# Two feed-forwards interleaved with a state scan: order of the scan's loads and of the first silu, and the place of a sum over weights

## The reference, cut to what matters

```python
x = x + tanh(g_ffn[0]) * L0_ffn(layernorm(x))   # stage 1: silu(gate) * up, two largest of each four kept, down
x = x + tanh(g_xattn[1]) * L1_xattn(...)        # stage 2
x = x + tanh(g_ffn[1]) * L1_ffn(layernorm(x))   # stage 3: h = silu(g * gate_s) * (u * up_s); down * down_s
x = x + tanh(g_xattn[2]) * L2_xattn(ctx, layernorm(x))  # stage 4: gates the result of the scan below
x = x + tanh(g_ffn[2]) * L2_ffn(layernorm(x))   # stage 5: weights rounded to fp8
# L2_xattn: for each of 16 states n, over time t
state = state * exp(delta_t * A[n]) + (delta_t * u_t) * B_t[n];   y_t += state * C_t[n]
# L3_ffn (stage 7) scales its weights by mean(|w|)
scale = 1.0 / clip(mean(abs(w)), EPS)
```

## Time and profile before

| | us |
|---|---|
| median of 3 runs | 4199.0 (4193.92 to 4204.99) |
| the profiled execution | 4200.43 |
| its span in the profile | 4198.9 |
| PE busy | 3734.7 (89%) |
| DVE busy | 3069.5 (73%) |
| ACT busy | 1683.8 (40%) |
| POOL busy | 669.8 (16%) |

### The profile page before, as it was taken

How to read it: one execution, slowest core, us unless ns; L and a number is a source line. 1 busy time by engine, 2 the same in 40 slices (tenths; PEclk the granted TensorE clock), 3 DMA queues, 4 the chain that set the end, 5 groups by cost and what they waited for, 6 DMA issues and landing times.

```text
span 4198.9 us, 41456 instructions
## 1 busy us (share of the span) xinstructions
PE 3734.7 (89%) x12733; PEld 1940.3 (46%) x12786; DVE 3069.5 (73%) x4986; ACT 1683.8 (40%) x2649; POOL 669.8 (16%) x647
## 2 busy tenths in 40 slices
PE   5988888989999998999984999899999999998656
PEld 3555655644444444444432444454554554553222
DVE  6787778768889788888898554575574673774887
ACT  4767676632333322433331011254352452551322
POOL 1433333433333110333210000000000000000000
PEclk8999999999999999999996999899999999999887
DMA  3323232424242322444432000221121110110000
GB/s 106 118 91 114 91 115 85 170 109 151 89 154 85 137 81 91 157 154 153 160 113 88 1 0 0 81 71 53 36 71 36 54 64 25 63 56 33 10 10 20
DMA packets 92131, 346.25 MB, mean 82 GB/s; under 512 B 12160, under 2 KB 20480, under 8 KB 78496
## 3 DMA queue, kind: packets, MB, share of 16 engines
q1 hardware_dynamic: 61888, 226.90, 15.1%
q0 software_dynamic: 30048, 116.94, 8.0%
HBM read 281.40 MB, written 62.39 MB: 82 GB/s over the span
## 4 chain that ended last, share of the span: by engine, by line
PE 55%; DVE 25%; issue 10%; ACT 6%; DMA 3%; POOL 0%; DVEq 0%; ACTq 0%; SPq 0%; POOLq 0%
PE ps L994 36%; PE ps L1339 5%; PE ps L1068 4%; PE ps L1329 3%; PE ps L1216 2%; DVE room L1491 2%; PE ps L1164 2%; DVE room L1495 2%; PE ps L1061 1%; DVE room L1499 1%; DMA room<-bc_scratch 1%; DVE stat L1453 1%; DVE room L1504 1%; DVE stat L1955 1%; DVE room L1960 1%
## 5 line engine op out<-in xcount | busy, mean ns | idle before, releaser
L994 PE MATMUL ps<-room 128*128 128x512 bf16 (+1 forms) x2873 | 955.7, 490 | 99.3 <-ACT room L942 49.0
L994 PE MATMUL ps<-lnT,room 128*128 128x512 f32 x2240 | 990.5, 598 | 22.6 <-DVE room L1685 8.1
L590 POOL TENSOR_TENSOR idle<-idle 128x1 f32<-128x1 f32 x288 | 477.8, 1659 | 1502.2 <-ACT room L795 553.3
L994 PEld LDWEIGHTS ps<-lnT,room 128*128 128x128 f32 x2240 | 427.2, 192 | 570.3 <-issue 534.7
L994 PEld LDWEIGHTS ps<-room 128*128 128x128 bf16 (+1 forms) x2912 | 401.2, 141 | 623.8 <-issue 329.0
L1164 PE MATMUL ps<-room 128*128 128x512 f32 x864 | 379.0, 596 | 8.5 <-DVE room L1637 8.5
L669 ACT ACTIVATE room<-room,small 128x511 f32<-128x511 f32 x256 | 163.6, 709 | 367.1 <-DVE room L1495 354.8
L994 PE MATMUL ps<-down_rows,room 128*128 128x256 f32 x1024 | 250.2, 400 | 47.5 <-ACT room L789 45.2
L1552 DVE TENSOR_TENSOR_SCAN room<-room 128x2048 f32<-128x2048 f32 x64 | 283.2, 4424 | 6.2
L1495 DVE TENSOR_TENSOR_SCAN room<-room 128x2048 f32<-128x2048 f32 x64 | 283.4, 4428 | 5.4
L1919 DVE TENSOR_REDUCE stat<-ps 128x1 f32<-128x512 f32 x256 | 177.1, 692 | 131.8 <-PE ps L994 131.8
(11 more groups left out here) (217 smaller groups left out, 4912.3 us busy)
## 6 DMA issues: line engine op xcount, KB each, us to landing
kv_stash<-room POOLq DMA_DIRECT2D x128, 256.0 KB, 2.7
room<-in_ffn SPq DMA_DIRECT2D x16, 2048.0 KB, 10.9
room<-bc_scratch POOLq DMA_DIRECT2D x128, 256.0 KB, 3.6
room<-kv_stash SPq DMA_DIRECT2D x64, 512.0 KB, 3.5
room<-stash POOLq DMA_DIRECT2D x24, 1024.0 KB, 9.5
room<-in_ffn SPq DMA_DIRECT2D x20, 1024.0 KB, 5.0
room<-in_ffn SPq DMA_DIRECT2D x12, 1536.0 KB, 7.9
room<-bc_scratch SPq DMA_DIRECT2D x64, 256.0 KB, 3.7
```

The costliest lines, as they stand in the source:

```text
L590: nc.gpsimd.tensor_tensor(idle[:, :], idle[:, :], idle[:, :], ALU.add).then_inc(zeros_added, 1)
L994: last = nc.tensor.matmul(out, lhsT, rhs, start=(i == 0), stop=(i == len(parts) - 1))
```

## The change

POOL: s_delta and s_du of batch 0 are loaded at the start, without a wait. In a batch, their waits and loads for the next batch stand after the loads of the last state's B and C and before the wait for the last addition to y. The waits are on the last decay and the last dBu of the batch. The counts of the marks follow (`WAITS` counts as before, less two in the last batch).

ACT: the decay of state 0 stands after the silu of tile 0.

The sums of |w|: DVE makes them in the third feed-forward instead of the second, the first three after the first group's cut of batches 1 to 3, the last after the third group's cut of batch 3. SP issues their loads after the loads of that stage, each but the first after the sum before it, into `e_bit`, which lies in the ring over the first slot of `e_raw`, once the last pieces are rounded.

```diff
-        f_bit, (f_tmp, f_ds) = arena[:, 2 * S:2 * S + BIT_CHUNK], split(arena[:, 10 * S:15 * S], 4 * D, D)
+        f_tmp, f_ds = split(arena[:, 10 * S:15 * S], 4 * D, D)
...
-        e_tmp = ring[:, 2 * SLOT2:]
+        e_tmp, e_bit = ring[:, 2 * SLOT2:], ring[:, 0:BIT_CHUNK]
...
# SP, ffn
-                    if s == 1:
-                        if not isinstance(b, int):
-                            sp.wait_ge(b_wabs, b)
-                        sp.dma_start(f_bit, bit_d[:, bass.ds(b * BIT_CHUNK, BIT_CHUNK)]).then_inc(b_abs_loaded, 16)
# SP, ffn8
+                sp.wait_ge(w_rounded, TILES[2] - EARLY)
+                for c in range(B):
+                    if c:
+                        sp.wait_ge(b_wabs, c)
+                    sp.dma_start(e_bit, bit_d[:, c * BIT_CHUNK:(c + 1) * BIT_CHUNK]).then_inc(b_abs_loaded, 16)
# POOL, feed_states
+                pool.dma_start(s_delta, stashed(0, 0)).then_inc(s_delta_loaded, 16)
+                pool.dma_start(s_du, stashed(1, 0)).then_inc(s_du_loaded, 16)
+
                 def body(b, last):
-                    before = b * WAITS + (s * B * WAITS + B * KV_WAITS)
-                    wait(s_dA_ready, state(s, b, 0), before)
-                    pool.dma_start(s_delta, stashed(0, b)).then_inc(s_delta_loaded, 16)
-                    wait(s_dBu_ready, state(s, b, 0), before + 1)
-                    pool.dma_start(s_du, stashed(1, b)).then_inc(s_du_loaded, 16)
-                    wait(s_y_stored, b * 16 + s * B * 16, before + 2)
+                    before = b * WAITS + (s * (B * WAITS - 2) + B * KV_WAITS)
+                    wait(s_y_stored, b * 16 + s * B * 16, before)
                     pool.dma_start(s_y, stashed(2, b)).then_inc(s_y_loaded, 16)
                     for j in range(STATES):
...
-                    wait(s_y_added, state(s, b, STATES), before + (WAITS - 1))
+                    at = before + (1 + 2 * STATES)
+                    if not last:
+                        wait(s_dA_ready, state(s, b, STATES), at)
+                        pool.dma_start(s_delta, stashed(0, b + 1)).then_inc(s_delta_loaded, 16)
+                        wait(s_dBu_ready, state(s, b, STATES), at + 1)
+                        pool.dma_start(s_du, stashed(1, b + 1)).then_inc(s_du_loaded, 16)
+                    wait(s_y_added, state(s, b, STATES), at + (0 if last else 2))
                     pool.dma_start(stashed(2, b), s_y).then_inc(s_y_stored, 16)
# ACT, ffn
                 def body(b, last):
-                    state_decay(s, b, 0)
                     for t in range(T):
...
-                        for j in range(1, STATES):
-                            if scan_tile(T, j - 1) + 1 == t:
+                        for j in range(STATES):
+                            if (scan_tile(T, j - 1) + 1 if j else 0) == t:
                                 state_decay(s, b, j)
# DVE, ffn
-                        if s == 1 and g == 2:
-                            dve.wait_ge(b_abs_loaded, b * 16 + 16)
-                            v.tensor_reduce(stat[:, bass.ds(b + 120, 1)], f_bit, AX.X, ALU.add, apply_absolute_value=True
-                                            ).then_inc(b_wabs, 1)
# DVE, ffn8
+                def sum_abs(c):
+                    dve.wait_ge(b_abs_loaded, c * 16 + 16)
+                    v.tensor_reduce(stat[:, bass.ds(c + 120, 1)], e_bit, AX.X, ALU.add, apply_absolute_value=True
+                                    ).then_inc(b_wabs, 1)
...
                         cut(t3(e_hT[g % 2], 3), e_h).then_inc(e_h_split, 1)
+                        if g == 0 and not first:
+                            sum_abs(b - 1)
+                        if g == 2 and last:
+                            sum_abs(B - 1)
```

More of the change, by code:

```diff
@@ L626, in body @@
                         n = s * STATES + j
-                        wait(s_dBu_ready, state(s, b, j), before + (3 + 2 * j))
+                        wait(s_dBu_ready, state(s, b, j), before + (1 + 2 * j))
                         pool.dma_start(s_B, bc_row(1, b, n)).then_inc(s_B_loaded, 16)
-                        wait(s_hC_ready, state(s, b, j), before + (4 + 2 * j))
+                        wait(s_hC_ready, state(s, b, j), before + (2 + 2 * j))
                         pool.dma_start(s_C, bc_row(1, b, DS + n)).then_inc(s_C_loaded, 16)
-                    wait(s_y_added, state(s, b, STATES), before + (WAITS - 1))
+                    at = before + (1 + 2 * STATES)
[5 more added lines that the diff above has]
+                    wait(s_y_added, state(s, b, STATES), at + (0 if last else 2))
                     pool.dma_start(stashed(2, b), s_y).then_inc(s_y_stored, 16)
```

## The result

| | median us | runs | profiled execution | its span |
|---|---|---|---|---|
| before | 4201.70 | 4 (4193.92 to 4204.99) | 4200.4 | 4198.9 |
| changed | 4172.91 | 4 (4164.61 to 4175.53) | 4164.61 | 4163.0 |

The ratio is 0.9931, 95% interval 0.9910 to 0.9951: 28.8 us less by the medians. Forecast were 4157 and a range of 4151 to 4171. The sign was right, the size too large; the median lies 1.9 us above the range, at the upper end of my rival 1 (4168 to 4173). The profiled execution is the fastest of its four, so its times flatter the change a little.

A forecast was written before the change was run, and what follows sets the result against it. PE bounds the first and third feed-forwards, nothing the second, where the gain must come from: batches of 118.6, 117.0, 117.0, 103.2 sum to 455.8 against 498.3, so 4200.4 - 42.5 = 4157.9, said as 4157; range 4151 to 4171.

The forecast's parts named there:

- rival 1: Second feed-forward, batch change: B row still needs 8.4 to 10 us; gain 27 to 32, time 4168 to 4173; chance 0.12.
- Loads ahead, POOL's chain: Second feed-forward, batch change: B issued 16.6 us after tile 10's product starts, landed at 21.6, ending the new chain.
- B row, 5.0 from its neighbours: Second feed-forward, batch change: B's row lands about 5.0 us after issue, with only the y load ahead.
- Tile 0's product at H + 16.8, transposes 1.9: Second feed-forward: next batch's first product 16.8 us after tile 10's product starts; transposes take 1.9 us instead of 3.63.
- State 7's B: Second feed-forward, dBu of state 7: of the 3.36 us wait 1.1 stays in batch 0, 0 in later batches.
- rival 2: Second feed-forward: state 7's B waits stay; 8.5 us in all not gained, time 4166; chance 0.10.
- Sums and their load: Second feed-forward: removing the sums saves 4.4 us in each of four batches; batch 0's state 7 wait falls 2.3.
- Sums in the third feed-forward, loads and silu in the first, at 0: Third feed-forward: four 4.4 us sums cost 0; first: moved loads and silu cost 0, within 1 us either way.
- Rival 4: Third feed-forward: the sums cost 4 to 17.6 us there, time 4162 to 4175; chance 0.07.
- Silu first, cost 0: ACT, second feed-forward: at most one more table load per batch, 1.3 us, covered by PE's up product; cost 0.
- PE under it, 115.4: Second feed-forward: PE's work per batch is 115.4 us, 116.9 with waits, just under the 117.0 chain.
- rival 3: Second feed-forward: PE is the bound, 121.2 us per batch at worst, time up to 4169; chance 0.12.

The follow-up runs named there:

- c0_after: The changed kernel, unaltered, measured and profiled a second time; 4173.3 us, ratio 0.9937.
- e2: The changed kernel with the sums of |w| and their load back in the second feed-forward; 4183.3 us, ratio 0.9967.
- e11: The changed kernel, SP's group 1 weights for the next batch held until B of that batch's state 0 has landed; 4158.3 us, ratio 0.9910.
- e1: The kernel before with only the sums of |w| moved to the third feed-forward; 4176.8 us, ratio 0.9949.
- e6: The changed kernel, group 1's gate and up weights held until y is stored, its down behind them; 4171.5 us, ratio 0.9932.
- e9: e3 with the next batch's group 0 gate and up weights held until B of the batch's last state has landed; 4151.2 us, ratio 0.9892.
- e4: The changed kernel with ACT's old order, first decay of a batch ahead of the first silu; 4171.5 us, ratio 0.9935.
- e5: The kernel before with only the first silu of a batch put ahead of the first decay; 4197.4 us, ratio 1.0002.
- e10: e3 with the weight waits of both e8 and e9; 4149.8 us, ratio 0.9886.
- e3: The changed kernel with B and C of the next batch's state 0 asked for ahead of the store of y; 4156.5 us, ratio 0.9900.
- e8: e3 with group 1's weights of the next batch held until the store of y has landed; 4153.7 us, ratio 0.9897.

## Why the prediction was wrong, point by point

- **Loads ahead, POOL's chain: the step that failed.** "The store no longer shares the DMA engines with delta and du: I take H + 16.6." I counted what left the store's company and not what arrived. Measured for B's issue in the first profile: H + 21.7, then 19.0 and 18.5, since the store landed in 9.6, 7.0 and 7.1 us. The first dBu came at H + 27.2, 24.3, 23.7 instead of 21.6: 5.6 + 2.7 + 2.1 = 10.4 of the 12.5 us that the stage missed. In `c0_after` it is 4.9 + 4.3 + 1.8 = 11.0 of 16.8. `e2` and `e11` show the cause from both sides: with the weights earlier, or later than B, the same chain gives 20.7 to 22.6.
- **Why the weights came.** Two halves that I costed one by one act on each other. The sum was 4.4 us and more of slack between PE's down product, which releases SP's loads, and the store of y. It went, and the store moved up to the weights: 8.9 us behind them instead of 15.3, and behind group 1's down instead of ahead of it. `e1` shows it without any load ahead (store 8.0, 5.0, 7.0 for 5.1, 5.2, 4.7). Which of the two transfers of group 1 costs how much stays open: `e6` and `e11` hold both back, and no run moves one alone. The traces speak for both: the down alone in `e1`'s third change (7.0), the gate and up in the changed kernel's second and third, where they land 2.2 and 1.7 us after the store is asked for, du 3.4 and 3.0 us after, and the down comes 1.1 and 0.7 us behind it (7.0, 7.1).
- **B row, 5.0 from its neighbours:** 5.4 and 5.1 measured, 5.0 in `e11`. Right, in part by luck: I took 5.1 us over "some 2.5 MB ahead", but SP had asked for 4 MB by then, 0.5, 2 and 1.5 at 1776.22, 1776.59 and 1777.22. Over 4 MB the same working gives 4.2.
- **Tile 0's product at H + 16.8, transposes 1.9:** 17.1, then 18.5 and 18.1 in the first profile, 17.2, 16.7 and 16.8 in `c0_after`; 1.91. Right, but for up to 1.7 us in the first profile, which B's lateness covers.
- **State 7's B, "1.1 stays in batch 0; in later batches 0":** 1.35, 0.79, 1.25 in the first profile, but 1.25, 2.94, 3.02 in `c0_after`. Batch 0 right, the later ones wrong: the weights were not through. This is the second term that failed, about 6 of the 16.8 us that `c0_after`'s stage missed. That is rival 2 in part, and `e9` confirms its cause (gate and up weights of the next batch's group 0 beside that row).
- **Sums and their load:** forecast were 17.6 for the sums and 8.5 for the waits at state 7 (2.3 + 3.1 + 3.1); `e1` shows 19.7 in all. The 17.6 and batch 0's 2.2 are right, the rest did not come. **Sums in the third feed-forward, loads and silu in the first, at 0:** right within what runs differ by. Rival 4 and rival 6 fell.
- **Silu first, cost 0:** its cost is 0, and so is its worth (`e4`, `e5`). I had named it in the cause of the 10.39 us without saying that B is late there by itself.
- **PE under it, 115.4:** 115.05 in `e10`. Right; rival 3 was not reached by the change.
- **Rival 1** had the price: "gain 27 to 32, time 4168 to 4173", because "next weights fall on it"; measured were 29.9 and 25.6 in the stage. Its place was one transfer off, the store and not the B row. I gave it 0.12 with the argument that two of three 1 MB loads leave; by `e2` those two alone cost the store nothing that can be seen, though they add 1.3 to 1.6 us once the weights are beside it (`e1` against the changed kernel). The trace held the means to see it: SP's issues stood at 1800.26 and 1800.70, released by PE, and the sum held up H (1805.03) but not them; and its third, at 1816.54, stood only 1.0 us behind the store.
- **A small transfer beside a large one.** State 7's B in batch 0, 256 KB on POOL's queue, took 3.7 us in `e9` without the 1.5 MB on SP's and 7.2 in `e3` with them; state 0's took 9.4 in `e6`. As the trace of before had it, a small transfer is not spared. The Trainium skill (DMA: Bandwidth & Descriptors, Queues, rings and completion order) has each DMA engine take packets from its queue rows in turn; these runs don't bear out what I had drawn from it for the landing of a whole B row. For the 1 MB store, 4.2 to 5.1 us against up to 9.6 in the changed kernel, a turn each, about twice the time, would fit; the 10.1 to 11.5 of `e9` lie above it, and no run shows the turns themselves.

## What to carry to other kernels

When work is taken off an engine, ask which transfers were released by another engine and now stand closer to those that this engine starts: the time removed may have been the gap that kept them apart. Write the issue times of all queues relative to the moved point, before and after the shift, and not only of the transfers that the change touches. And where an idle time names one releaser, look for the next one just behind it: removing one of two waits that end together gives nothing.

## What the runs showed of the hardware

The company that counts is what is unfinished when a transfer is asked for, or is asked for just before it. The 1 MB store of y landed in 4.1 to 4.2 us after the last batch, where nothing is beside it, and in 4.5 to 5.1 in `e2`, with two 1 MB loads asked for on its own queue 5.5 and 10.4 us earlier, of which the second landed 0.4 us before to 0.8 us after the store was asked for. With 1.5 MB on SP's queue unfinished for 4.9 us more and 0.75 MB asked for 0.3 us ahead it took 9.6. What is on its own queue seems to count as well: in `e8` and `e10`, with group 1's weights held back but a C row asked for 0.7 us ahead and du unfinished for another 2.4 to 3.6 us, it took 5.8 to 6.7.

POOL's operation on one element per partition, 0.18 us by itself, lasts until the large operation of DVE that it meets is over, here the scan from 1797.66 to 1802.07. POOL's timeline of the changed kernel:

```profile
1797.65 4.40 POOL L591 TENSOR_TENSOR idle<-idle 128x1 f32<-128x1 f32 x1
```

A load behind such a mark is asked for that much later; in `e3` (3.11 us of it) DVE then waited for y.
